# Cross attention and FFN with low-rank experts on one core: the first tile's column correction taken from PSUM, four-byte fillings, and a second normalisation by logarithm, exponential and a Newton step

## What is computed

```python
q1 = fake_quant(layernorm(x), s1, z1)         # x: 2 x 512 x 1024; q = clip(round(v/s + z), 0, 255); (q - z) * s
q2 = fake_quant(ctx, s2, z2)                  # ctx: 2 x 1024 x 1024
x  = x + q1 @ q2
u  = layernorm(x)
gate = u @ gate_w.T                           # 8 experts, the best 2 with softmax weights
low  = u @ lora_A.T                           # rank 16 for each expert
x  = x + u @ base_w.T + base_b + 2 * sum_e w_e * (low_e @ lora_B_e.T)
```

## Time and profile before

| | |
|---|---|
| median of 3 runs | 168.84 us (168.42 to 168.93) |
| profiled execution, its own time | 169.07 us |
| its span | 167.1 us |
| TensorE busy | 158.9 us, 95%, 824 matmuls |
| VectorE busy | 110.9 us, 66% |
| ScalarE busy | 82.3 us, 49% |
| GpSimd busy | 35.0 us, 21% |
| granted TensorE clock | 1.00 of 2.4 GHz |
| TensorE's share of the chain that ended last | 82% |

### The profile page before, as it was taken

The page is one execution under the profiler, slowest core; times in us unless marked ns, Lnnn a source line. Parts: engine busy times, 40 slices in busy tenths (PEclk is TensorE's granted clock), DMA queues, the critical chain, the costliest instruction groups (busy, mean ns, idle before and its releaser), DMA issues.

```text
span 167.1 us, 2359 instructions
## 1 busy us (share of the span) xinstructions
PE 158.9 (95%) x824; PEld 121.0 (72%) x824; DVE 110.9 (66%) x250; ACT 82.3 (49%) x107; POOL 35.0 (21%) x69
## 2 busy tenths in 40 slices
PE   5859998999999999999999999999999999999993
PEld 2224544788888768887868768878888888998882
DVE  6976688989989979999493927584750364322061
ACT  3089978872675556265357094446325544330000
POOL 3334026130731201403720520012071000000000
DMA  5999999949989999003995599951969993000024
GB/s 214 312 418 419 408 411 411 230 79 326 365 192 274 310 239 357 19 0 63 197 179 92 105 178 193 320 187 16 145 120 201 195 269 126 4 0 0 0 87 166
DMA packets 22045, 32.68 MB, mean 196 GB/s; under 512 B 13714, under 2 KB 13970, under 8 KB 22034
## 3 DMA queue, kind: packets, MB, share of 16 engines
q1 hardware_dynamic: 20016, 25.20, 46.9%
q0 software_dynamic: 2016, 7.34, 23.7%
q10 hardware_dynamic: 2, 0.00, 0.0%
HBM read 22.05 MB, written 4.19 MB: 157 GB/s over the span
## 4 chain that ended last, share of the span: by engine, by line
PE 82%; DVE 6%; DMA 4%; POOL 2%; ACT 2%; issue 1%; SPq 0%; DVEq 0%; ACTq 0%; POOLq 0%
PE ps_odd L1083 24%; PE ps_even L1083 20%; PE ps_att L1028 11%; PE ps_g L1064 5%; DMA x_sb<-in_ctx 4%; PE ps_t L1008 2%; PE ps_g L1067 2%; PE ps_even L1116 2%; PE ps_even L1118 2%; PE ps_even L1117 2%; PE ps_odd L1028 2%; PE ps_even L1036 2%; DVE x_sb L724 1%; POOL r_v L381 1%; PE ps_odd L1145 1%
## 5 line engine op out<-in xcount | busy, mean ns | idle before, releaser
L1083 PE MATMUL ps_odd<-w_hi,yt 128*128 128x512 f32 x128 | 38.4, 407 | 0.0
L1028 PE MATMUL ps_att<-c,c1t 128*128 128x512 f16 x96 | 31.4, 383 | 0.0
L1083 PE MATMUL ps_even<-w_hi,yt 128*128 128x512 f32 x96 | 27.7, 401 | 0.0
L1083 PEld LDWEIGHTS ps_odd<-w_hi,yt 128*128 128x128 f32 x128 | 23.7, 189 | 5.0 <-issue 0.2
L1064 PE MATMUL ps_g<-ag,yt 128*128 128x272 f32 x64 | 21.2, 375 | 0.0
L1083 PEld LDWEIGHTS ps_even<-w_hi,yt 128*128 128x128 f32 x96 | 17.9, 188 | 3.6
L1083 PE MATMUL ps_odd<-w_lo,yt 128*128 128x512 f32 x64 | 20.0, 401 | 0.0
L518 ACT ACTIVATE y_words<-yt_planes 128x1024 uint16<-128x1024 uint16 x8 | 10.3, 1353 | 14.1 <-DMA yt_planes<-y_planes 14.1
L1083 PE MATMUL ps_even<-w_lo,yt 128*128 128x512 f32 x48 | 15.1, 406 | 0.0
L718 DVE SCALAR_TENSOR_TENSOR x_sb<-ps_att,q_ss,x_sb 128x512 f32<-128x512 f32 x12 | 8.4, 746 | 9.6 <-PE ps_att L1028 6.6
L445 ACT ACTIVATE qc<-ring,q_in,q_rec 128x1024 uint16<-128x1024 f32 x11 | 13.3, 1231 | 1.6 <-issue 1.6
(11 more groups left out here) (142 smaller groups left out, 297.0 us busy)
## 6 DMA issues: line engine op xcount, KB each, us to landing
ring<-in_ctx SPq DMA_DIRECT2D x12, 512.0 KB, 7.4
x_sb<-in_x SPq DMA_DIRECT2D x8, 512.0 KB, 8.3
w_raw<-in_w_t SPq DMA_DIRECT2D x8, 512.0 KB, 11.4
x_sb<-in_base_b POOLq DMA_DIRECT2D x8, 512.0 KB, 8.1
out_x<-x_sb SPq DMA_DIRECT2D x15, 256.0 KB, 2.4
x_sb<-zfix POOLq DMA_DIRECT2D x6, 512.0 KB, 6.8
x_sb<-in_ctx SPq DMA_DIRECT2D x4, 512.0 KB, 7.6
ag_raw<-in_ag_t SPq DMA_DIRECT2D x1, 544.0 KB, 13.1
```

Of the source, the lines that this page charges most:

```text
L1028: ins = pe.matmul(att_bank(t)[h][:, :], c1t[:, t % 4, k, :], c2[:, k, h * HALF:(h + 1) * HALF], start=(k == 0), stop=(k == CT - 1))
L1083: pe.matmul(ffn_bank[t % 2][h][:, :], rows_of(part, t, k), w[:, k, h * HALF:(h + 1) * HALF], start=start, stop=False)
```

## The change

1. Tile 0's column correction: add_columns on VectorE adds ssd1 * colsum straight from PSUM to x tile 0, before its attention is added; ssdd, a constant for each row, goes into rowfix(0). The halves are taken in turns: VectorE half 0 while ScalarE makes zfix half 1, then the other way round. add_zfix is left for tile 1 alone, and variance(1, 0) follows add_attention(0).
2. Tiles 0 and 1: rstd is no longer made by GpSimd. first_guess(t) on ScalarE computes exp(-0.5 * ln(var + eps)), and normalise_x1(t) refines it with one Newton step in three small VectorE operations. GpSimd's rstd_x1(0) and rstd_x1(1) are gone.
3. byte_ones fills c1 as 512 four-byte elements in place of 1024 two-byte ones.
4. All five lists are put in a new order. Loads: context 1 and 2 behind x(2), ag behind w(0) and w(1), w(6) and w(7) ahead of x(4), load_b behind transpose_c1(4), store(0, 0) earlier. TensorE keeps the same calls; transpose_y(0, 0) and (0, 1) stand together behind attention(3, 4, 1), low_and_gate of tile 0 starts behind base_high(0, 1), and so on.

```diff
+TWO_ONES = struct.unpack("<f", struct.pack("<HH", 0x6400, 0x6400))[0]
...
 # ScalarE
+            def first_guess(t):
+                act.wait_ge(var_ready[1], t + 1)
+                act.wait_ge(eps_ready, 1)
+                act.activation(ln_v[:, t:t + 1], mv[:, 1, t, 1:2], ACT.Ln, bias=eps[:, :]).then_inc(logv_ready, 1)
+                act.wait_ge(logv_ready, t + 1)
+                act.activation(r0[:, t:t + 1], ln_v[:, t:t + 1], ACT.Exp, scale=-0.5).then_inc(guess_ready, 1)
...
             def zero_point_row(t):
+                if t == 0:
+                    act.activation(rowfix[:, t:t + 1], rowsum[:, t:t + 1], ACT.Identity, bias=ssdd,
+                                   scale=ssd2).then_inc(rowfix_ready, 1)
+                    return
...
             def zero_point_columns(b):
-                for h in range(2):
+                for h in (1, 0) if b == 0 else (0, 1):
+                    if b == 0 and h == 0:
+                        act.wait_ge(columns_taken, 1)
...
             take_c1t(2)
             zero_point_columns(0)
             scale_x(3)
+            take_c1t(3)
+            first_guess(0)
+            split_ag_hi()
             split_w_hi(0)
-            take_c1t(3)
             split_w_hi(1)
+            split_y_hi(0, 0)
             split_w_hi(2)
-            split_y_hi(0, 0)
-            split_w_hi(3)
             split_y_hi(0, 1)
-            split_ag_hi()
-            split_w_hi(4)
-            scale_context(8)
-            split_w_hi(5)
+            for k in range(3, 6):
+                split_w_hi(k)
+            first_guess(1)
             split_w_hi(6)
...
 # VectorE
             def byte_ones(t):
-                dve.memset(c1[:, t, :], BYTE_ONE).then_inc(bytes_ready, 1)
+                dve.memset(c1[:, t, :].bitcast(F32), TWO_ONES).then_inc(bytes_ready, 1)
...
+            def add_columns():
+                dve.wait_ge(colsum_psum, 1)
+                dve.wait_ge(ss_ready, 1)
+                dve.wait_ge(qx_ready[0], 2)
+                for h in range(2):
+                    if h == 1:
+                        dve.wait_ge(zfix_ready, 1)
+                    cols = slice(h * HALF, (h + 1) * HALF)
+                    dve.scalar_tensor_tensor(out=x_sb[:, 0, cols], in0=ps_even[h][:, :], scalar=ssd1,
+                                             in1=x_sb[:, 0, cols], op0=ALU.mult, op1=ALU.add).then_inc(columns_taken, 1)
...
             def normalise_x1(t):
-                dve.wait_ge(rstd_ready, t + 1)
+                if t < 2:
+                    g = r0[:, t:t + 1]
+                    dve.wait_ge(guess_ready, t + 1)
+                    chain(dve.tensor_scalar(r_v[:, 1, t:t + 1], mv[:, 1, t, 1:2], EPS, g, ALU.add, ALU.mult))
+                    chain(dve.tensor_scalar(r_h[:, t:t + 1], r_v[:, 1, t:t + 1], g, -0.5, ALU.mult, ALU.mult))
+                    chain(dve.tensor_scalar(rstd[:, 1, t:t + 1], r_h[:, t:t + 1], 1.5, g, ALU.add, ALU.mult))
+                else:
+                    dve.wait_ge(rstd_ready, t - 1)
...
             variance(0, 3)
+            add_columns()
+            x_shift(3)
             add_attention(0)
-            x_shift(3)
-            add_zfix(0)
             variance(1, 0)
-            split_w_lo(0)
+            add_attention(1)
             normalise_x1(0)
-            add_attention(1)
+            split_ag_lo()
             split_y_lo(0, 0)
-            add_zfix(1)
+            add_zfix()
             split_y_lo(0, 1)
             variance(1, 1)
-            split_ag_lo()
+            split_w_lo(0)
             normalise_x1(1)
...
 # GpSimd
-            square_constants()
-            x_scale(0)
-            x_scale(1)
             scale_product()
-            x_scale(2)
+            square_constants()
             quant_constants()
-            x_scale(3)
-            rstd_x1(0)
+            for k in range(0, 4):
+                x_scale(k)
             add_zfix(2)
             add_zfix(3)
-            rstd_x1(1)
+            rstd_x1(2)
             add_bias(0)
...
 # TensorE, attention of tile 2 and the order around the first output matmuls
                     if t == 2:
-                        pe.wait_ge(zfix_ready, 2)
+                        pe.wait_ge(columns_taken, h + 1)
+                        pe.wait_ge(zfix_ready, 2 - h)
...
             attention(3, 4, 0)
+            attention(3, 4, 1)
+            transpose_y(0, 0)
             transpose_y(0, 1)
-            attention(3, 4, 1)
+            attention(2, 6, 1)
             attention(3, 5, 0)
+            attention(2, 7, 0)
             attention(3, 5, 1)
-            for k in range(0, 5):
+            attention(2, 7, 1)
+            base_high(0, 0)
+            base_high(0, 1)
+            for k in range(0, 3):
+                low_and_gate(0, k)
+            base_high(0, 2)
+            low_and_gate(0, 3)
+            for k in range(3, 6):
                 base_high(0, k)
-            for k in range(0, 4):
-                low_and_gate(0, k)
             transpose_y(1, 0)
```

More of the change, by code:

```diff
@@ L870, in _ @@
+            cut_context(8)
             split_w_lo(2)
             split_w_lo(3)
-            x_shift(4)
-            split_y_lo(1, 1)
-            weigh_low(0)
             cut_x(4)
-            add_attention(3)
             split_w_lo(4)
             split_w_lo(5)
+            cut_context(9)
+            split_w_lo(6)
+            weigh_low(0)
+            split_w_lo(7)
             normalise_x1(2)
-            cut_context(8)
-            cut_context(9)
             top_logits(1)
-            split_w_lo(6)
@@ L884, in _ @@
-            split_w_lo(7)
             split_b_lo()
+            cut_context(10)
             split_low_lo(0)
-            cut_context(10)
             weigh_low(1)
+            finish_tile(0)
+            split_low_lo(1)
             cut_context(11)
+            split_y_lo(2, 0)
+            variance(1, 3)
+            sum_context(1)
             cut_context(12)
-            split_y_lo(2, 0)
-            finish_tile(0)
+            sum_context(2)
+            variance(0, 5)
+            sum_context(3)
@@ L933, in _ @@
             add_attention(6)
+            variance(1, 6)
+            top_logits(4)
             finish_tile(3)
-            top_logits(4)
-            variance(1, 6)
+            normalise_x1(6)
             weigh_low(4)
@@ L1201, in _ @@
             attention(2, 1, 1)
+            attention(1, 7, 1)
             attention(2, 2, 0)
+            transpose_c1(3)
             attention(2, 2, 1)
@@ L1255, in _ @@
-            base_high(1, 6)
-            base_low(0, 1)
-            base_low(0, 2)
-            base_high(1, 7)
-            for k in range(0, 3):
-                base_low(1, k)
+            low_and_gate(0, 4)
+            attention(3, 6, 1)
+            low_and_gate(0, 5)
+            attention(3, 7, 0)
+            base_high(0, 6)
+            base_high(0, 7)
+            low_and_gate(0, 6)
+            transpose_y(1, 1)
+            attention(3, 7, 1)
+            low_and_gate(0, 7)
+            base_low(0, 0)
@@ new lines, in _ @@
+            base_high(1, 0)
+            base_low(0, 1)
+            for k in range(1, 4):
+                base_high(1, k)
+            for k in range(0, 6):
+                low_and_gate(1, k)
+            base_low(0, 2)
+            for k in range(4, 8):
+                base_high(1, k)
+            base_low(0, 3)
+            base_low(0, 4)
+            base_low(1, 0)
+            base_low(0, 5)
+            base_low(1, 1)
+            low_and_gate(1, 6)
+            attention(4, 0, 0)
+            base_low(1, 2)
@@ L1272, in _ @@
+            attention(4, 1, 1)
             lora(0, 0)
             lora(0, 1)
-            attention(4, 1, 1)
-            base_low(1, 5)
+            transpose_low(1)
             attention(4, 2, 0)
+            base_low(1, 6)
+            base_low(1, 7)
             attention(4, 2, 1)
-            transpose_low(1)
+            lora(1, 0)
+            lora(1, 1)
+            transpose_y(2, 1)
             attention(4, 3, 0)
-            base_low(1, 6)
+            low_and_gate(2, 0)
             attention(4, 3, 1)
-            transpose_y(2, 1)
+            base(2, 0)
@@ L1295, in _ @@
+            attention(4, 5, 0)
+            transpose_y(3, 0)
+            attention(4, 5, 1)
             low_and_gate(2, 4)
```

402 lines of the change are left out of this document (191 added, 211 removed).

## The result

| | before | after |
|---|---|---|
| median, 5 runs each | 168.84 us (168.42 to 168.93) | 167.99 us (167.52 to 168.16) |
| ratio, 95% interval | | 0.9947 (0.9928 to 0.9967) |
| a second time, with the experiments | 168.92 us | 167.81 us, ratio 0.9943 (0.9927 to 0.9959) |
| span of the profiled execution | 167.1 us | 166.1 us |
| last matmul starts | 164.02 us | 163.06 us |

The kernel is faster by 0.5 to 0.6%, 0.85 us in the first comparison and 1.11 in the second. The forecast was 168.2 us (167.4 to 169.4), with 0.52 on faster.

A forecast was written before the change was run, and what follows sets the result against it. TensorE bounds the kernel, unbroken from 40 us, with waits before that. Terms of -0.3, -0.34 and -0.23 sum to -0.87 us, plus 0.2 for hand-overs: 168.84 - 0.67 = 168.2 us, range 167.4 to 169.4.

The forecast's parts named there:

- Start and context tiles: Up to column_sums_first(7): attention(0, 0, 0) starts about 1.1 us earlier, given back waiting for contexts; column_sums_first(7) stays near 20.6.
- Column correction: Tile 0: attention(2, 0, 0) at 23.05, some 0.45 us of TensorE lost; mv(0) at 25.8 instead of 26.25.
- Second normalisation: Tile 0's Ln, Exp and Newton step: y(0) from 27.7, 0.70 us wait gone, ScalarE late next; base_high(0, 0) -0.3 us.
- The hold: GpSimd seems held while VectorE subtracts two SBUF tensors; x_scale(4)'s first op takes 0.34 us, not 2.23.
- Tile 1: At transpose_y(1, 0): y(1) ends at 36.4, TensorE arrives at 37.1, so the wait goes: -0.34 us.
- The rest of the list: TensorE's list: low_and_gate calls standing behind another go from 21 to 16, 5 x 0.045 = -0.23 us.
- Loads: Moved loads cost nothing; x(4) goes out earlier, at about 32, which covers contexts 9 to 12.
- Tight hand-overs, +0.2: Waits possible at low_and_gate(1, 0), lora(0, 0), transpose_low(1), lora(1, 0) and behind x_scale(4): +0.2 us, bounds 0 and 1.6.
- rival C: Whole kernel: slips are nil, 168.0 us, down to 167.4 if half of the start's 1.1 us stays; chance 0.20.
- A: ScalarE's queue: Ln starts 0.4 us later, tight hand-overs take another 0.2 to 0.4; 168.4 to 169.1 us; chance 0.30.
- B: load_b, moved behind transpose_c1(4), comes late for lora(0, 0); a load of 7.4 us gives 170.3 us; chance 0.10.
- D: ScalarE: Ln is not in the loaded table, more table loads put 2.6 us in front of w_hi; 170.5 us; chance 0.02.

The follow-up runs named there:

- Experiment 8: After, with context 1 and 2 loaded ahead of x(2) again, the engines' lists left as in after: 168.99 us, ratio 0.9997 to before.
- Experiment 5: After, with tile 0's column correction as before (zfix by ScalarE, add_zfix(0) on VectorE, x_shift(3) behind add_attention(0)): 168.29 us, ratio 0.9976 to before.
- experiment 2: After, with rstd for tiles 0 and 1 made by GpSimd again in place of first_guess on ScalarE: 167.47 us, ratio 0.994 to before.
- experiment 1: Before, with the logarithm, exponential and Newton step for tiles 0 and 1 alone, in the old order: 168.75 us against 168.76, ratio 1.0001.
- experiment 3: Before, with VectorE's order alone changed: add_attention(1) ahead of normalise_x1(0), split_w_lo(0) behind normalise_x1(1): 169.34 us, ratio 1.0048.
- Experiment 4: Before, with add_attention(1) ahead of normalise_x1(0), split_w_lo(0) in split_w_lo(1)'s slot, split_w_lo(1) and split_y_lo(1, 1) behind variance(0, 4): 167.85 us, ratio 0.9956.
- experiment 7: After, with 13 more low_and_gate calls of tiles 4 and 5 standing behind another one, attention calls between them moved behind: 168.29 us, ratio 0.996 to before.
- experiment 12: Experiment 2, with 11 low_and_gate calls of tiles 0, 1, 6 and 7 taken apart by base_high, base_low, base or base_last calls: 171.01 us, ratio 1.0161 to before.
- experiment 10: Experiment 2, with attention(1, 7, 1) ahead of attention(2, 0, 0) and split_w_hi(1) moved behind split_y_hi(0, 0): 168.36 us, ratio 0.9978 to before.
- experiment 6: After, with the two-byte fillings of c1 in place of the four-byte ones: 168.03 us, ratio 0.9946 to before.

## Why the prediction was right

The sign, the two waits that go and the size within 0.4 us (168.2 forecast, 167.99 and 167.81 measured) held; the reason given for the second normalisation did not. That the size came so near is in part luck: the forecast had too much gain at base_high(0, 0), a loss at hand-overs that didn't come, and too little gain in the rest of the list, where 0.3 us have no cause shown.

- **Start and context tiles.** column_sums_first(7) was said to stay near 20.6 and is at 20.71; attention(0, 0, 0) came 0.62 us earlier (11.71 to 11.09), not 1.1, and this was given back as stated. The other 0.5 is VectorE's new order: take_first(0) stands ahead of cut_context(0), so column_sums_first(0) started at 10.39 and not at 9.89 as the prediction had it. Experiment 8 shows that the order of the lists and of the loads belong together: with one of them undone 1.1 us are lost at this place. Against before nothing is won there (12.57 for 12.46 behind context 0).
- **Column correction.** mv(0) at 25.92 for 25.8; attention(2, 0, 0) at 23.08 for 23.05, with a wait of 0.26 us for the 0.45 lost in the forecast. Experiment 5 shows that the whole edit pays (0.34 us at base_high(0, 0)), but through x_shift(3) and transpose_c1(3), a path that the prediction doesn't have. The prediction counts twelve plus fourteen attention matmuls up to transpose_y(0, 0); the list has 24, and its 28.7 is the time of 24.
- **Second normalisation: right times, wrong credit.** y(0) ran from 27.85 (27.7 forecast), the transpose came at 28.82 (28.7), split_y_hi at 29.48 (29.4), base_high(0, 0) at 30.90 (30.8): 0.21 won for 0.3. ScalarE was named as what is late next; it wasn't: in experiment 2, without Ln and Exp in its queue, ScalarE stood 0.43 us ahead of y's copy and base_high(0, 0) came no earlier (22.75). TensorE's own list up to the transpose is the bound there. And the part was costed as the logarithm's and Newton step's doing, and experiments 1 and 2 show that these bring nothing, either alone or in place. What went is the w_lo subtraction from between variance and y: it took 1.17 us of VectorE, and held GpSimd's add for 1.04 in place of 0.19. The prediction named this hold from the earlier trace rows but didn't ask what GpSimd would need once w_lo was moved: 0.19 + 0.56, as little as the replacement. In experiment 1 w_lo still stands ahead of y, so the faster rstd has nothing to bring forward.
- **The hold.** The forecast of 0.34 for x_scale(4)'s first operation, not the 2.23 of before, held: 0.33. Where rstd_x1's add starts beside add_attention, with one operand in PSUM, it takes 0.19 us in every trace. Just behind the start of one subtraction of SBUF tensors it takes 1.04 or 1.05 us (w_lo) and 1.10 or 1.11 (ag_lo, in before and in experiments 3 and 4), and x_scale's first operation beside two of them 2.23. The rule of the Trainium skill (SBUF — State Buffer, "SBUF: two separate sides"), a lock on a shared port pair, agrees with these rows. They are not the only long ones: later in after an add takes 1.23 us, and its end, 68.10, lies just behind that of VectorE's y at 68.05:

```profile
66.87 1.23 POOL L386 TENSOR_SCALAR r_v<-mv,q_sq 128x1 f32<-128x1 f32 x1 [1.72 <-DVE mv L691]
```

- **Tile 1.** The wait at transpose_y(1, 0) is gone, as said (-0.34). y(1) ended at 36.52 for 36.4; the transpose came at 37.45 for 37.1, since the matmuls ahead of it cost more, not because it waited. Experiment 4, with the old order here, still has this wait.
- **The rest of the list.** From base_high(0, 0) to the last matmul it took 132.68 us before and 131.93 after: 0.75 less, of which 0.34 are tile 1's wait. At experiment 7's price the 5 pairs are 5 x 0.035 = 0.18, not 0.23, and by experiment 12 even that is too much: of the five calls only three now stand behind an attention (25 before, 28 after, counted in the two kernels), the other two behind a base call, which saves nothing. 3 x 0.035 is about 0.1 us, an estimate. The other 0.3 us I can't assign: the order of the narrow and wide matmuls changed in many places. This term stays open.
- **Loads.** x(4) was said to go out at about 32; it went at 36.70, as good as before (36.87). Its zfix DMAs were issued earlier, at 23.26 and 24.88 against 28.03, but the load waited for them to land until 36.7. Attention of tile 4 waits for nothing even so.
- **Tight hand-overs, +0.2.** Not spent: no wait of TensorE from 30.90 us on. This is why the time came out below the forecast; with this term nil the sum was rival C's 168.0, and that is near what was measured, though other terms of it were off both ways. It was right to keep such a term: experiments 3, 10 and 12 each lost 0.3 to 2.2 us at one hand-over.
- **Fillings.** 0.48 us for 0.46. What they are worth on the path is below what experiment 6 can tell.
- **Rivals.** A: the slips of ScalarE's queue were 0.1 us, not 0.4. B: load_b landed at 53.83 (53.9 forecast), and lora(0, 0) started at 58.67 without a wait. (Its border of 6.7 us is reckoned on the sum without the +0.2; on 168.2 it is 6.5.) D: the Ln took 0.29 and the Exp 0.20 us, and the trace has one table load, as before.

The sum by terms, behind context 0: -0.22 (forecast -0.3) at base_high(0, 0), -0.34 (-0.34) at tile 1, -0.41 (-0.23) in the rest, 0 (+0.2) for hand-overs: -0.97 (-0.67).

No version beats after by more than can be measured. Experiment 2 equals it (154.70 against 154.68 and 154.75 us) and does without the logarithm, the Newton step and their four small tiles, so it is the one to keep.

## What to carry to other kernels

When a small operation on GpSimd looks slow, look first at what VectorE does beside it: once a subtraction with both operands in SBUF had been moved away, replacing GpSimd's work by two other engines brought nothing more. After a call is moved out of the critical place, find the place where it does no harm: the same idea was worth -0.60 us with the displaced calls laid out well and +0.61 with them put in a row. In lists written by hand the loads and all engines' orders are one piece; the moves of loads, scale_x, x_shift, w_hi and low_and_gate each cost 0.3 to 3 us at the first call whose cover they took away, so before moving a call earlier ask which buffer it overwrites and who reads that last.

## What was not expected of the hardware

The stream of loads runs full or dips at its start, from one execution to the next. Rate of the DMA in 40 slices from 1.5 to 9 us, after's first trace, then experiment 2's (the same loads):

```profile
GB/s 0 197 131 175 284 371 415 437 371 437 393 371 437 350 415 393 328 328 284 218 240 240 284 284 262 153 262 328 415 437 371 328 371 350 371 371 415 393 393 459
```
```profile
GB/s 0 197 153 153 218 371 393 306 415 393 481 437 371 371 371 415 437 372 350 371 415 415 371 393 393 415 459 393 393 415 437 437 393 350 415 481 481 372 350 415
```

From about 4.5 to 7 us the first falls to 153 to 328 GB/s, the second stays near 400. ScalarE could start on context 0 at 8.15 in the first and 7.17 in the second:

```profile
8.15 1.24 ACT L460 ACTIVATE qc<-x_sb,q_in,q_rec 128x1024 uint16<-128x1024 f32 x1 [5.60 <-DMA x_sb<-in_ctx]
```
```profile
7.17 1.24 ACT L462 ACTIVATE qc<-x_sb,q_in,q_rec 128x1024 uint16<-128x1024 f32 x1 [4.62 <-DMA x_sb<-in_ctx]
```

The whole trace behind it lies 1 us earlier. After's own second trace has the early start too (7.14), and its runs spread from 167.05 to 168.41, wider than the whole gain. What makes the dip stays open. The count from context 0 leaves out one thing: in the six traces with context 1 and 2 loaded ahead of x(2) ScalarE started on context 0 at 8.10 to 8.39, in the eight with x(2) first at 7.09 to 8.15. Whether the order of the loads helps there, or it is chance, no run here separates. A comparison of two single traces of this kernel that doesn't take this start out would read 1 us of luck as an effect.
